# Loops over chunk numbers unpacked from one table word, on VectorE and TensorE

## The reference

```python
src, dst = edge_index                                   # 200000 edges, 6250 nodes, dst sorted
agg = jax.ops.segment_sum(x[src], dst, num_segments=N)  # [6250, 256]
h = jax.nn.relu(agg @ W_rel + b_rel + x @ W_root)       # [6250, 512]
gates = h @ W_ih.T + b_ih + b_hh
i, f, g, o = jnp.split(gates, 4, axis=-1)
c = jax.nn.sigmoid(i) * jnp.tanh(g)
h_lstm = jax.nn.sigmoid(o) * jnp.tanh(c)
x = _layernorm(x + h_lstm @ W_fc + b_fc, axis=-1)
```

## Time and profile before

| | |
|---|---|
| median of 3 runs | 1879.01 us (1873.73 to 1880.08) |
| profiled execution, its own time | 1876.59 us |
| its span | 1874.6 us |
| mean granted TensorE clock | 0.889 |
| PE busy | 1478.7 us (79%) |
| DVE busy | 776.2 us (41%) |
| ACT busy | 393.2 us (21%) |
| POOL busy | 1360.6 us (73%) |
| HBM | 178 GB/s over the span |
| chain that ended last | POOL 37%, issue 28%, PE 24% |

### The profile page before, as it was taken

How to read it: one execution, slowest core, us unless ns; L and a number is a source line. 1 busy time by engine, 2 the same in 40 slices (tenths; PEclk the granted TensorE clock), 3 DMA queues, 4 the chain that set the end, 5 groups by cost and what they waited for, 6 DMA issues and landing times.

```text
span 1874.6 us, 32527 instructions
## 1 busy us (share of the span) xinstructions
PE 1478.7 (79%) x6531; PEld 1182.2 (63%) x6532; DVE 776.2 (41%) x1635; ACT 393.2 (21%) x720; POOL 1360.6 (73%) x2094
## 2 busy tenths in 40 slices
PE   0046576677688878988868999888798999999887
PEld 0023354455577767766656887767576888887766
DVE  8666535455322123454453132444544222333222
ACT  0000011121211022323212122332222122322223
POOL 3866778877777777777777777757776767567770
PEclk9985676788799988988888999899988999999999
DMA  7944555555576766555656776645555766556660
GB/s 248 350 136 126 150 170 150 154 171 153 167 233 206 225 180 180 170 158 172 174 171 194 231 233 187 174 128 163 166 160 158 247 190 197 154 160 178 179 177 17
DMA packets 132286, 334.47 MB, mean 178 GB/s; under 512 B 18527, under 2 KB 63228, under 8 KB 130534
## 3 DMA queue, kind: packets, MB, share of 16 engines
q0 software_dynamic: 81984, 267.98, 49.1%
q10 hardware_dynamic: 46248, 48.38, 8.2%
q1 hardware_dynamic: 3936, 16.62, 2.3%
HBM read 313.70 MB, written 19.20 MB: 178 GB/s over the span
## 4 chain that ended last, share of the span: by engine, by line
POOL 37%; issue 28%; PE 24%; DVE 3%; DVEq 3%; POOLq 2%; DMA 1%; ACT 0%; SPq 0%; ACTq 0%
POOL rows L382 27%; PE ps_blk L516 10%; POOL idx L352 9%; PE ps_agg L455 4%; PE ps_y L524 2%; PE ps_win L443 2%; PE ps_blk L498 2%; PE ps_blk L503 2%; POOL rows L367 1%; POOLq L352 1%; DVEq L872 1%; PE ps_win L430 1%; DVE hot_key L877 1%; PE ps_tr L430 1%; DMA rows<-x_parts,idx 1%
## 5 line engine op out<-in xcount | busy, mean ns | idle before, releaser
L382 POOL DMA_INDIRECT rows<-x_parts,idx x1008 | 1032.6, 1024 | 416.5 <-POOL idx L352 164.3
L455 PE MATMUL ps_agg<-rows,onehot 128*125 x1204 | 379.5, 469 | 231.8 <-SPq L321 112.5
L516 PE MATMUL ps_blk<-cell,wih_sb 128*128 128x250 f32 x2400 | 555.0, 390 | 3.2 <-issue 2.1
L516 PEld LDWEIGHTS ps_blk<-cell,wih_sb 128*128 128x128 f32 x2400 | 470.4, 198 | 74.1 <-issue 11.2
L455 PEld LDWEIGHTS ps_agg<-rows,onehot 128*125 128x125 f32 x1204 | 257.4, 220 | 318.3 <-issue 261.7
L886 DVE SCALAR_TENSOR_TENSOR onehot<-iota_f,tile_first,dst_u 128x500 f32 x301 | 224.0, 746 | 279.5 <-PE ps_agg L455 154.7
L352 POOL COPY idx<-src_sb 128x1 int32 x1040 | 280.8, 270 | 15.7 <-issue 8.8
L643 ACT ACTIVATE cell<-ps_blk,bg_sb 128x250 f32<-128x250 f32 x300 | 140.8, 470 | 565.3 <-PE ps_blk L516 445.4
L872 DVE TENSOR_SCALAR rel<-key,span_key x213 | 52.0, 244 | 290.8 <-issue 196.4
L430 PE MATMUL ps_tr<-hot_key,hot_lo 128*128 x344 | 75.7, 341 | 91.1 <-issue 56.9
L877 DVE TENSOR_TENSOR hot_key<-iota_h,rel 128x980 f16 x213 | 141.0, 662 | 0.1
(11 more groups left out here) (120 smaller groups left out, 830.1 us busy)
## 6 DMA issues: line engine op xcount, KB each, us to landing
hot_key<-in_xb ACTq DMA_DIRECT2D x21, 896.0 KB
rows<-x_parts,idx POOLq DMA_INDIRECT x1008
x_t<-in_xT ACTq DMA_DIRECT2D x25, 250.0 KB
x_n<-in_x ACTq DMA_DIRECT2D x25, 250.0 KB
out<-y ACTq DMA_DIRECT2D x25, 250.0 KB
x_parts<-wih_sb SPq DMA_DIRECT2D x4, 1024.0 KB, 6.9
wih_sb<-in_x ACTq DMA_DIRECT2D x6, 512.0 KB, 8.1
x_parts<-cell SPq DMA_DIRECT2D x2, 1024.0 KB
```

What stands on the lines that cost most here:

```text
L382: g.indirect_dma_start(rows_f[:, k * QC + j, :], None, x_parts, bass.IndirectOffsetOnAxis(ap=idx[:, k, j:j + 1], axis=0)).then_inc(landed[ ...
L455: ins = mm(o, onehot[:, hot * QC + j, 0:TN], rows[:, ds(slot + j, 1), :].squeeze(1), start=(first and j == 0), stop=False)
L516: last = mm(o, wih_sb[:, k, col:col + P], h_t[:, k, :], start=(k == 0), stop=(k == KH - 1))
```

## The change

Each table word now holds the first chunk times 2048 plus a number just past the chunk number of the last pair. Both engines unpack it with plain register operations after a load without bounds, and loop from the first number to that end in steps of four, so that the loop's number is the chunk number. The running pair number and its place modulo 4 stay in registers that are advanced in the loop: the place by one, multiplied by whether it is still below four. The table's arithmetic has two more linked operations.

```diff
-PACK = 1024
+PACK = 2048
...
+        def unpack(engine, regs, at):
+            packed, first, past = regs
+            engine.reg_load(packed, table[0:1, at:at + 1] if isinstance(at, int) else table[0:1, ds(at, 1)])
+            engine.reg_alu(first, packed, PACK, ALU.python_divide)
+            engine.reg_alu(past, first, -PACK, ALU.mult)
+            engine.reg_add(past, past, packed)
+            return engine.snap(first, min_val=0, max_val=CHUNKS - 1), engine.snap(past, min_val=1, max_val=CHUNKS)
+
+        def next_pair(engine, pair, place, more):
+            engine.reg_add(pair, pair, 1)
+            engine.reg_add(place, place, 1)
+            engine.reg_alu(more, place, PAIRS, ALU.is_lt)
+            engine.reg_alu(place, place, more, ALU.mult)
...
-                        packed = pe.value_load(table[0:1, ds(at, 1)] if not isinstance(w, int) else table[0:1, at:at + 1], min_val=1, max_val=CHUNKS * PACK)
-                        pe.reg_mov(n_span, packed % PACK)
-                        n = pe.snap(n_span, min_val=1, max_val=STEPS)
-                        s0 = pe.snap(pair_0, min_val=0, max_val=MAX_PAIRS)
                         o = bank[:, side * SCOLS:(side + 1) * SCOLS]
-                        with pe.Fori(0, n) as m:
-                            s = pe.snap(s0 + m, min_val=0, max_val=MAX_PAIRS)
-                            half = pe.snap(s % PAIRS, min_val=0, max_val=PAIRS - 1)
+                        first, past = unpack(pe, pe_regs, at)
+                        with pe.Fori(first, past, QC):
+                            s = pe.snap(pair_0, min_val=0, max_val=MAX_PAIRS)
+                            half = pe.snap(place, min_val=0, max_val=PAIRS - 1)
                             pe.wait_ge(pairs_ready, s + 1)
...
                             last.then_inc(pairs_summed, 1)
-                        pe.reg_add(pair_0, pair_0, n)
+                            next_pair(pe, pair_0, place, more_places)
...
             link(v.tensor_copy(hi, row_i[:, 0:SPANS]))
+            link(v.scalar_tensor_tensor(hi, hi, float(QC), lo, ALU.mult, ALU.add))
+            link(v.tensor_scalar(hi, hi, -float(QC - 1), None, ALU.add))
             link(v.scalar_tensor_tensor(table[:, T_SPAN:T_SPAN + SPANS], lo, float(PACK), hi, ALU.mult, ALU.add))
...
-                packed = dve.value_load(table[0:1, at + T_SPAN:at + T_SPAN + 1] if static else table[0:1, ds(at + T_SPAN, 1)], min_val=1, max_val=CHUNKS * PACK)
-                dve.reg_mov(low, packed // PACK)
-                dve.reg_mov(n_span, packed % PACK)
-                n = dve.snap(n_span, min_val=1, max_val=STEPS)
-                base = dve.snap(pair_0, min_val=0, max_val=MAX_PAIRS)
-                with dve.Fori(0, n) as m:
-                    s = dve.snap(m + base, min_val=0, max_val=MAX_PAIRS)
-                    c = dve.snap(m * QC + dve.snap(low), min_val=0, max_val=CHUNKS - 1 + QC)
-                    half = dve.snap(s % PAIRS, min_val=0, max_val=PAIRS - 1)
+                first, past = unpack(dve, dve_regs, at + T_SPAN)
+                with dve.Fori(first, past, QC) as c:
+                    s = dve.snap(pair_0, min_val=0, max_val=MAX_PAIRS)
+                    half = dve.snap(place, min_val=0, max_val=PAIRS - 1)
                     dve.wait_ge(pairs_summed, s + 1)
...
-                dve.reg_add(pair_0, pair_0, n)
+                    next_pair(dve, pair_0, place, more_places)
```

More of the change, by code:

```diff
@@ L403, in _ @@
             pair_0 = pe.alloc_register("pair_0")
-            n_span = pe.alloc_register("n_span")
+            pe_regs = [pe.alloc_register(name) for name in ("packed", "first", "past")]
+            place = pe.alloc_register("place")
+            more_places = pe.alloc_register("more_places")
+            pe.reg_mov(place, 0)
             pe.reg_mov(step_0, 0)
@@ L849, in _ @@
             group0 = dve.value_load(table[0:1, T_GROUP0:T_GROUP0 + 1], min_val=0, max_val=2 * STEPS)
-            low = dve.alloc_register("low")
-            n_span = dve.alloc_register("n_span")
+            dve_regs = [dve.alloc_register(name) for name in ("packed", "first", "past")]
+            place = dve.alloc_register("place")
+            more_places = dve.alloc_register("more_places")
+            dve.reg_mov(place, 0)
             step_0 = dve.alloc_register("step_0")
```

## The result

The changed kernel takes 1847.45 us (median of 4 runs, 1844.77 to 1848.42), against 1878.68 of the kernel before beside it: ratio 0.9836, 95% interval 0.9815 to 0.9857, or 31 us less. The forecast was 1858.8 with a range of 1843 to 1872, so the direction and the range held, and the gain was half as large again as the forecast's sum of 20.2 us. The profiled execution took 1848.42 us with a span of 1846.6, 28 us less than the one of before.

A forecast was written before the change was run, and what follows sets the result against it. Gathers set the pace from 165 to 1190 us, VectorE the first slot, TensorE from 1190 to 1700. Terms -7.5 - 12.2 - 1.2 + 0.7 = -20.2 us took 1879.0 to 1858.8 us, range 1843 to 1872.

The forecast's parts named there:

- Where it pays: Two stretches, 116 to 160 and 1190 to 1440 us, can pay; the second dense group gives 1.2 us.
- VectorE, per pair: Steps inside a span in the first slot go from 1.52 to 1.26 us, 21 x 0.25 = 5.3 us.
- What stretched hot_lo: At 180 us hot_lo took 0.70 instead of 0.43, read as VectorE held up by something; a rule against the change.
- The first slot: At 116 to 160 us, VectorE's savings per pair and per span together give 7.5 us, all used by GpSimd.
- TensorE, per span: In the third dense group's two-window slots, 0.25 us less sequencer time per span; 9 x 4 x 0.25 = 9.0 us.
- VectorE's lateness: Part sums' waits for onehot after 1190 us, beyond TensorE's own load, are VectorE being late: 1.7 us gained.
- The clock comes back: Rival: shorter idles halve the half-clock loss of gate matmuls in nine slots, 11.7 us more gain, 1847.1; chance 0.15.
- The table: Two more linked operations on 150 columns delay GpSimd's first index, adding 0.7 us.
- The steps don't shrink: Rival: contention or a dearer next_pair loses VectorE's step gain, 5.3 us less, 1864.1; chance 0.13.
- Only one place pays: Rival: TensorE's sequencer held until gates drain, part sums stay late, steps don't shrink; 1871.8 us; chance 0.05.
- Tests stay: Rival: bounds given to the snaps bring the range tests back in both engines' loops; 1879.7 us; chance 0.07.
- Slower through holds: Rival: unexplained 1.4 us sequencer holds recur in span loops; with 25 of them 1893.8 us; chance 0.05.

The follow-up runs named there:

- e11: Changed kernel with the range test of c alone back on VectorE, kept alive by an added zero register; ratio 0.9864 to the kernel before.
- e1: Changed kernel with TensorE's old code back and a second, old-form table word per span; ratio 0.9931 to the kernel before.
- e9: Changed kernel with range test and assert of the table loads back on both engines; ratio 0.9936 to the kernel before.
- e10: Kernel before without its tests, unpacking words by division, multiplication and addition, chunk and pair numbers in growing registers; ratio 0.9820 to the kernel before.
- e2: Changed kernel with VectorE's old code back and both forms of the table word; ratio 0.9950 to the kernel before.
- e12: Changed kernel with modulo pair place, TensorE's words loaded between the gates' thirds, and GpSimd's index copies two visits ahead; 2011 us, ratio 1.0730.
- e7: Changed kernel with modulo pair place and TensorE's slot words loaded and unpacked between the thirds of the gates; 1837.7 us, ratio 0.9781.
- e8: Changed kernel with modulo pair place and slot words loaded early on TensorE (among gates) and VectorE (ahead of one-hots); ratio 0.9805.

## Why the prediction was right or wrong

- **Where it pays: right.** The first slot and the third dense group paid, and GpSimd's waits took it up in full: 61.9 to 32.7 us. The second dense group gave nothing (285.2 us between the fifth and the ninth last layer before, 286.3 after), at the low end of the 0 to 2.4 given for it. What TensorE saved there came out as waits for the landing of gathers, as the reading that gathers set the pace had it; before from 724 to 1080, then after from 714 to 1074:

```profile
PE ps_agg L455 <- SPq L321: 15.3, 7, 4.2
...
PE ps_agg L469 <- SPq L335: 44.9, 13, 5.4
```

- **VectorE, per pair: right in kind, too small.** The floor of 1.26 was wrong. It was taken as the 1.53 at 180 us less the 0.27 by which one operation had stretched; rel and hot_lo start 0.14 apart when the instructions are there in time, and the pair takes 1.16. The test of c has 0.33 in the step; e11 puts it, with an addition, at 0.39 (1.55 against 1.16).
- **What stretched hot_lo: wrong.** The 0.70 us at 180 was read as VectorE held up by something. It isn't: in every one of the 14 traces the same 84 of the 213 pairs have a hot_lo of 0.67 us or more, and the other 129 one of 0.52 or less, whatever GpSimd does at the time. Worked out from the input's edges, the 84 are exactly the pairs whose span starts at a chunk with an odd number, so that the slice of src_lo (float16) starts at an odd element. In the first slot all four spans start at even chunks (0, 44, 62, 76), and all 25 are short; in the third group both kinds stand:

```profile
L887 DVE TENSOR_TENSOR hot_lo<-iota_h,src_lo x25: 411/426/517, 119.1 to 148.3; 128x512 f16 x25
...
1193.73 0.69 DVE L887 TENSOR_TENSOR hot_lo<-iota_h,src_lo 128x512 f16 x1
```

- **The first slot: 7.5 forecast, 10.5 measured.** Of this 6.3 us of lead are left at gather 144 in e1 (whose slot is 8.2 us shorter), 8.7 in the changed kernel, each with a start that was over 2 us late.
- **TensorE, per span: the term that was mis-sized.** 0.25 was taken (0.1 to 0.35), 0.43 measured in the slot shown. Of it, the load's test and assert are 0.33 (e9) where 0.25 stood in the step: a move goes with them, and the division behind them takes 0.21 instead of 0.18. The rest is not pinned down: the old loop has a move and two additions of 0.03 us each, with gaps, that the step did not count, but e10, which keeps the old loop, is at 1.91 us a span, so the loop's shape is the small part. 0.18 x 42 is 7.6 us of the missing gain.
- **VectorE's lateness, 1.7 us: wrong.** It was read as waits for onehot beyond what TensorE's own load costs. e2 shows that without VectorE's part TensorE keeps 10.7 of 24.7 us. That these 10.7 are close to the 10.5 forecast for TensorE's spans is luck: each span was shortened by 0.43 and not by 0.25, and VectorE, left as it was, took back the difference. Waits are charged to the last of two late engines, and the one that is just behind has no row.
- **The clock comes back: a part.** It had 0.15 and 11.7 us. The granted clock did rise, from 0.91 to 0.94, and 1010 matmuls took 6.2 us less, with a scatter of some 3. By the sign given for it the rival came true, as the gates behind the slot of the earlier trace rows take 5.33 us after 7.83, but not in nine slots: of the 16 groups of gates in the four turns before, two were slow, 7.83 and 6.46 us, and all gates together are 2.5 us shorter. One row had been taken for nine. The median of 1847.45 us is where this rival had it (1847.1), and that is a coincidence: of the 12.5 us that the forecast was short in the third group, these matmuls are half, and the other half is idle time that went with the sequencers' work.
- **The table: 0.7 forecast,** 0.4 measured at the first gather of all, one execution of each kernel.
- **Against the other rivals.** *The steps don't shrink:* no. GpSimd was gathering in the first slot, and hot_lo stayed at a median of 0.43 us with 0.52 at most. The exclusive lock that the Trainium skill describes for some operations of VectorE (SBUF — State Buffer, section "SBUF: two separate sides") is not seen at the pitch of 1.16, so these three operations give no sign of it here, and the 0.70 has another cause. *Only one place pays:* no, both did; but each engine alone pays only a third (e1 0.7%, e2 0.5% of 1.6%). *Tests stay:* no assert is left at the lines of the span loops. *Slower through holds:* the longest load on VectorE is now 1.31 us, and no such loss is seen in this kernel. e12 has holds of 20 us and more on VectorE; whether they are of the same kind is not known.

In sum, -20.2 became -28.2 in the profiled executions. By turns, TensorE is 4.2 us ahead when the third group begins and 28.9 when it ends: 24.7 instead of 12.2 there. That gap is 7.6 us for the span's price and 6.2 for the shorter matmuls, 13.8 against the 12.5 that were missing, an agreement within the chance of some 4 us in each profile. Ahead of it, the slot's 10.5 shrank to 4.2 through the late start (2.7) and the waits for landings; waits for batches of x are 2.3 us there.

## What to carry to other kernels

Range tests of loaded and computed register values are paid per loop turn in the sequencer: where spans are short (four matmuls), doing without two kinds of them gave 1.8% here (e10), and the reshaped loops and the kept modulo register nothing that can be measured; try the tests alone first. Where two engines feed each other at nearly the same pitch, look at the pitch of both before costing either: in the third group shortening one gave 3.0 or 10.7 us, shortening both 24.7. Loads of table words that the sequencer can do behind a long run of matmuls cost nothing there (e7); on VectorE, ahead of one-hots that TensorE waits for, they did (e8). Before a stretched instruction is called contention, check whether it is the same instruction in every trace: if so, look at its operands.

## What the runs showed that I had not expected

- 0.70 us more per span on TensorE's sequencer cost 38.4 us, of which 15.9 were longer matmuls, at a granted clock of 0.88 instead of 0.94.
- hot_lo takes 0.43 or 0.69 us by whether its float16 slice starts at an even or an odd element, in the same 84 of 213 pairs in all 14 traces.
- Small matmuls in the idles raised the granted clock in all 12 executions (0.898 to 0.909 against 0.882 to 0.892) and did not shorten the kernel.
- A test of 0.16 us and an assert of 0.02 on TensorE lengthen a span by 0.33.
- VectorE's three operations of a pair (0.23, 0.43 and 0.66 us) fit into 1.16 when they come in time, less than the 1.32 of their sum: they overlap.
- Index copies one visit earlier on GpSimd took 117 us of its waits for them away and made the kernel 7% slower, with VectorE held up to 38.6 us by something that the trace calls remote.
